# Edge-maximum passes of a graph network: which engine makes the first key tile of a layout step

## The reference, cut to what matters

```
def _sage_pool_layer(x, src, dst, Wp, bp, Ws, Wn, b, n_nodes):
    m = jax.nn.relu(x @ Wp + bp)
    msgs = m[src]
    agg = jax.ops.segment_max(msgs, dst, num_segments=n_nodes)
    agg = jnp.where(jnp.isfinite(agg), agg, 0.0)
    return x @ Ws + agg @ Wn + b
...
# third layer; its weighted sum uses a node-by-node matrix of edge weights
gathered = support[edge_col] * edge_val[:, None]
out = jax.ops.segment_sum(gathered, edge_row, num_segments=x.shape[0])
```

## Time and profile before

| | us |
|---|---|
| median of 3 runs | 2772.53 |
| lowest and highest | 2771.99, 2778.91 |
| the profiled execution, its own time | 2772.04 |
| its span in the trace | 2770.3 |
| first edge-maximum pass, in the trace | 662 to 1168 |
| second edge-maximum pass, in the trace | 1229 to 1740 |

### The profile page before, as it was taken

One profiled execution on the slowest core, in us unless ns is written; L12 is line 12 of the kernel. 1 busy time (PEld: TensorE's weight loads), 2 busy tenths in 40 slices (PEclk: granted clock), 3 DMA queues, 4 the chain that ended last, 5 costly groups with the idle time before them and its releaser, 6 DMA issues. The chain is left out here.

```text
span 2770.3 us, 72947 instructions
## 1 busy us (share of the span) xinstructions
PE 2500.8 (90%) x29568; PEld 2013.3 (73%) x29568; DVE 1823.9 (66%) x5033; ACT 1158.4 (42%) x2585; POOL 1280.8 (46%) x1575
## 2 busy tenths in 40 slices
PE   6998999996899999678999996479899999999999
PEld 3666777764666666446666665469899999999998
DVE  6997999987889888448889885310444444444444
ACT  5997888874444444324444444210411111111110
POOL 4007999983888888558888887310000000000000
PEclk8558999997999999689999997579999999999999
DMA  5103000004555555535555556369000000000000
GB/s 167 42 2 103 12 13 12 12 20 125 135 135 142 141 127 147 129 92 129 138 138 136 138 132 166 107 222 345 33 2 2 2 2 2 2 2 1 2 2 19
DMA packets 147301, 226.91 MB, mean 82 GB/s; under 512 B 55184, under 2 KB 113259, under 8 KB 146290
## 3 DMA queue, kind: packets, MB, share of 16 engines
q1 hardware_dynamic: 121502, 185.74, 22.4%
q0 software_dynamic: 21920, 35.15, 6.4%
q10 hardware_dynamic: 3540, 1.30, 0.2%
HBM read 121.74 MB, written 100.35 MB: 80 GB/s over the span
## 5 line engine op out<-in xcount | busy, mean ns | idle before, releaser
L1892 POOL DMA_INDIRECT max_row<-table,max_src_rows x608 | 656.2, 1079 | 173.3 <-issue 154.2
L1934 PE MATMUL max_far<-adj 128*96 128x512 f16 x2200 | 599.9, 386 | 8.0 <-DVE adj L2060 4.1
L2060 DVE TENSOR_SCALAR adj<-adj,node_numbers 128x512 f16<-128x512 f16 x1100 | 391.3, 376 | 122.6 <-PE max_far L1934 89.1
L1758 POOL TENSOR_SCALAR e<-e 128x512 f32<-128x512 f32 (+1 forms) x625 | 365.7, 604 | 178.4 <-ACT e L1746 160.8
L2405 PE MATMUL prop<-g,adj 128*128 128x192 f16 x4608 | 386.4, 247 | 9.4 <-DVE g L2479 9.4
L1772 DVE TENSOR_TENSOR e<-e,a_ps 128x1024 f32<-128x1024 f32 (+1 forms) x313 | 372.1, 1194 | 32.6 <-PE a_ps L1684 12.6
L2405 PEld LDWEIGHTS prop<-g,adj 128*128 128x128 f16 x4608 | 379.9, 98 | 14.1 <-issue 9.2
L2405 PE MATMUL prop<-weights_then_states,adj 128*128 128x192 f16 x4608 | 384.3, 246 | 0.0
L2405 PEld LDWEIGHTS prop<-weights_then_states,adj 128*128 128x128 f16 x4608 | 378.9, 98 | 3.7 <-issue 2.5
L1746 ACT ACTIVATE e<-s_ps 128x512 f32<-128x512 f32 (+1 forms) x625 | 335.4, 585 | 60.0 <-PE o_ps L1696 38.6
L1934 PEld LDWEIGHTS max_far<-adj 128*96 128x96 f16 x2200 | 255.6, 129 | 127.5 <-issue 14.9
(11 more groups left out here) (292 smaller groups left out, 3613.5 us busy)
## 6 DMA issues: line engine op xcount, KB each, us to landing
weights_then_states<-weights SPq DMA_DIRECT2D x100, 400.0 KB, 5.0
weights<-max_rows_w SPq DMA_DIRECT2D x52, 400.0 KB
rows_dram<-max_out SPq DMA_DIRECT2D x100, 192.0 KB
weights<-adj SPq DMA_DIRECT2D x48, 400.0 KB
max_same<-same_dram SPq DMA_DIRECT2D x196, 96.0 KB
rows_dram<-adj SPq DMA_DIRECT2D x96, 192.0 KB
max_row<-table,max_src_rows POOLq DMA_INDIRECT x608
adj<-ids_dram SPq DMA_DIRECT2D x44, 128.0 KB
```

The source lines that it names most:

```text
L1758: nc.gpsimd.tensor_scalar(e_tile(u), e_tile(u), math.exp(10.0), math.exp(-10.0), ALU.min, ALU.max).then_inc(clipped, 1)
L1892: nc.gpsimd.indirect_dma_start(row[i % RING][:, j, :], None, table_dram, bass.IndirectOffsetOnAxis(ap=src_rows[:, 4 * n + j:4 * n + j + 1] ...
L1934: mm = nc.tensor.matmul(far_ps[j % 2][0:D, :], parts[:, k, a, :], hot[(T * j + k) % HOTS], start=k == a == 0, stop=k == T - 1 and a == 1)
L2060: nc.vector.tensor_scalar(hot[i % HOTS], ids[j % 2], numbers[:, k:k + 1], None, ALU.is_equal).then_inc(hot_made, 1)
```

## The change

GpSimd makes the first key of step k only if k is below 3 or block k - 3 is gathered. The list `firsts` holds these 78 of 100 steps; the counts that GpSimd, TensorE and VectorE wait for are converted with `firsts_until`. In the 22 steps k with k - 3 in `FAR` (7, 11, ..., 91, all of them with 4 windows), VectorE makes the key of window 0 as well, into the buffer `key_hot[n % 2][:, 0]`, which was allocated before and not used. There are two passes, so 44 key tiles move. No DMA, buffer or matmul is added or removed.

```diff
@@
+        firsts = [k for k in range(PARTS) if k < AHEAD or k - AHEAD not in FAR]
+        firsts_until = lambda n: sum(k < n for k in firsts)
@@ GpSimd
             def first_key(k):
-                if k >= FIRSTS:
-                    pool.wait_ge(hots_used, k - FIRSTS + 1)
-                nc.gpsimd.tensor_scalar(first_key_hot[k % FIRSTS][:, 0:FEW_KEYS], columns, keys[:, first_win[k]:first_win[k] + 1], None, ALU.is_equal).then_inc(first_key_made, 1)
+                i = firsts_until(k)
+                if i >= FIRSTS:
+                    pool.wait_ge(hots_used, firsts[i - FIRSTS] + 1)
+                nc.gpsimd.tensor_scalar(first_key_hot[i % FIRSTS][:, 0:FEW_KEYS], columns, keys[:, first_win[k]:first_win[k] + 1], None, ALU.is_equal).then_inc(first_key_made, 1)
@@
-                if n + AHEAD < PARTS:
+                if n + AHEAD in firsts:
                     first_key(n + AHEAD)
@@ TensorE, lay_out
-                    hot_of = key_hot[n % 2][:, w, 0:FEW_KEYS] if w else first_key_hot[n % FIRSTS][:, 0:FEW_KEYS]
+                    by_pool = w == 0 and n in firsts
+                    hot_of = first_key_hot[firsts_until(n) % FIRSTS][:, 0:FEW_KEYS] if by_pool else key_hot[n % 2][:, w, 0:FEW_KEYS]
@@
-                    if w == 0:
-                        pe.wait_ge(first_key_made, n + 1)
+                    if by_pool:
+                        pe.wait_ge(first_key_made, firsts_until(n) + 1)
                     else:
-                        pe.wait_ge(hots_ready, first_win[n] - n + w)
+                        pe.wait_ge(hots_ready, first_win[n] + w + 1 - firsts_until(n + 1))
@@ VectorE, keys_of
-                for w in range(1, m):
+                for w in range(int(n in firsts), m):
```

More of the change, by code:

```diff
@@ L1894, in gather @@
                                              ).then_inc(gathered[j], 16)
-            for k in range(AHEAD):
-                first_key(k)
+            for k in firsts:
+                if k < AHEAD:
+                    first_key(k)
             for n in range(PARTS):
```

## The result

The changed kernel takes 2760.43 us in the median (2749.12 to 2771.19, 14 runs), the kernel before, timed beside it, 2773.70 (2765.84 to 2785.74, 14 runs). The ratio is 0.995 with a 95% interval of 0.9934 to 0.9965: 13.3 us faster, more than the 0.3% that a measurement can tell. That is in the range and on the side that was forecast, but 0.55 of the forecast gain of 24.3 us.

The account below looks back on a forecast made before the run. GpSimd's list bounds both passes, with TensorE close behind. First pass 13.1 - 1.5 - 1.0 = 10.6, second 15.2 - 0.5 - 1.0 = 13.7, together 24.3 us off 2772.5: 2748 us, range 2740 to 2764.

Parts of the forecast that it names:

- The bound: In both edge-maximum passes: GpSimd runs free, so a pass lasts its list plus a tail of some 9.5 us.
- The price of a key, 0.69 us net: GpSimd's list: a key's 0.804 us plus gaps 0.02 and 0.17, less the usual 0.30 between gathers, saves 0.69 us.
- 15.2 us per pass: GpSimd's list: 22 key tiles removed at 0.69 us each shorten each pass's list by 15.2 us.
- STEP: Follow-up theory: GpSimd, shorter per step, runs in step with VectorE; its keys come beside VectorE instructions that lengthen them.
- TensorE can follow by 13.1 and 15.2: TensorE gains only what it now waits for gathered rows: 13.1 us in the first pass, 15.2 in the second.
- The rival "TensorE": TensorE becomes the pace in the first pass: gains of 3 and 9 us, 12 us together, 2760; chance 0.18.
- VectorE 1.5 and 0.5 us: Price of the 22 added key tiles per pass on VectorE: 1.5 us in the first pass, 0.5 in the second.
- disturbance 1.0 per pass: The added 6.7 us of VectorE work lengthens GpSimd's work beside it, costing 1.0 us per pass.
- Lock: Rival: each added VectorE tile stops GpSimd for its whole 0.305 us; 15 us gained, 2757; chance 0.10.
- Transfers: Rival: landings of gathers set the rate, so GpSimd's saving returns as DMA waits; 0 to 5 us, 2770; chance 0.06.
- VectorE: Rival: VectorE becomes the pace, the moved tiles adding 13.4 us to the path; slower, 2786; chance 0.04.

## Why the prediction was right, and where its size was wrong

**The bound: right.** A pass lasts as long as GpSimd's list plus a tail of 9 to 10 us. It held in the first trace of the changed kernel (tails 9.2 and 10.4). Taking all keys off the list gave 109 us. Where ScalarE is late it holds less well: one of the two tails is longer in its second trace (13.2), in the second and third of before (14.1, 13.1) and with the scan later (15.2).

**The price of a key, 0.69 us net: near.** Where only the moved keys are left against none, the lists differ by 0.58 us per key; that the whole time gives 0.68 is luck in part. In the changed kernel the gap of 0.30 and the missing key are there as described.

**"15.2 us per pass": the step that failed in the first trace.** It multiplied the net price by 22 and took GpSimd's other instructions as they were. The lists became 6.4 and 6.6 us shorter: they lost 22 keys each, and the 75 kept ones between gathers went from 0.832 to 1.002 us and from 0.784 to 0.989, 28.1 us in both passes, more than the whole forecast. That so much of the gain was left is luck in part, since the gathers were shorter by 15 us. The prediction looked at disturbance only from the side of the added tiles, and the run without them shows that they do nothing. That the same 156 keys can take another length without any change to VectorE's list is shown by the key one gather earlier (800 ns, 983 in the changed kernel) and by the changed kernel itself, traced twice (983 and 765). What they meet is the lane products of `weigh`, in 53% of the keys, in 19 and 21% in the two short cases; this was read from what ran beside and not tried by itself, and what sets the place of the keys in VectorE's step is open. So STEP stands as a reading of these traces, and the run that was to try it from VectorE's side, the scan later, does not bear on it.

**"TensorE can follow by 13.1 and 15.2": two answers.** In the trace with long keys it was never asked, and its waits for rows rose (17.0 to 27.0). In the trace with short keys it could not: its waits for rows fell to 16.1 us in both passes, and GpSimd waited 21 us for it. There this is the step that failed: what TensorE stops waiting for is not what it gains, since it waited elsewhere instead, 45 us by "issue", in an execution with the late ScalarE. The rival "TensorE" had given 2760, and the two causes end at nearly the same time, so the median of 2760.4 is no proof of either. That it lies in the range is therefore not the prediction's sum coming true: the forecast gain was 11 us too large, by one step or the other.

**VectorE 1.5 and 0.5 us, disturbance 1.0 per pass: too high, at nothing.** Without the 44 tiles the time is 2763.95, no shorter than 2760.43.

**The rivals.** Lock: out, by the run without the tiles. Transfers: the waits for landings rose by 6.5 and 5.8 us, more than the 5 that I had named as its sign, but most gathers still wait for none; it became a wait of some size (62.6 and 62.4 us) only with all or most keys gone. VectorE: out, its waits for TensorE rose.

**Left open.** Why ScalarE starts late in some executions and in others never; one chip gave both kinds. It bears on the reading: the three traces of before have the lateness and the changed kernel's long keys come from one without. The nearest thing to a trace of before without it is that of both engines making the tiles, which has GpSimd's list of before, no lateness and keys of 807 ns; so without lateness too the keys are short with 200 and long with 156 at this place of the key (983 and, without the tiles, 997), and with it they are short with both (804 and 765 ns). How many of the 14 timed executions were of which kind is not known, so the gain of 13.3 us is a median over whatever mixture there was. Not settled either: why a list takes the phase it takes (the key behind gather 0 is worth 24 us with 156 keys and nothing with 200), and the 7.8 us of the kernel in which both engines make the tiles.

## What to carry to other kernels

When instructions leave the list of the engine that sets the pace, forecast the durations of those that stay as well as the number that goes: the kept ones may come to lie beside other work, which was worth here as much as the edit itself (0.30 to 1.06 us per moved key for the same edit at two places of one line). And a wait that shrinks on the next engine is a gain only if that engine does not wait elsewhere instead (40 us of waits for rows gone, some 3 to 10 us won). Ask first whether all of the helper work can leave that engine: the keys of the steps without gathers gave 13 us, all keys 109. And profile both kernels more than once before a difference in one kind of instruction is put down to the change.

## What the runs showed of the hardware that was not expected

- The same comparison of 128x125 on GpSimd takes from 0.59 to 2.48 us beside different work of the other engines; the mean over the keys of a pass lay between 0.74 and 1.06 us in these kernels. Wholly beside far comparisons of 128x512 on VectorE one took 0.63 us, and the comparison 0.84 instead of 0.34; the keys that met a lane product of `weigh` took 1.16 in the mean in the first trace of the changed kernel, the others 0.79. The gathers moved far less: 1.04 to 1.09 us.
- ScalarE is late by 117 to 194 us in total in five traces and by 0 in nine; the changed kernel has one of each, and its whole time does not tell them apart (2769.0 and 2765.8).
